# Transposing the input of a feed-forward stage on TensorE, or reading it turned from DRAM and sending the moments round through DRAM

## The reference

```python
def _layernorm(x, axis=-1, eps=1e-05):
    m = jnp.mean(x, axis=axis, keepdims=True)
    v = jnp.var(x, axis=axis, keepdims=True)
    return (x - m) / jnp.sqrt(v + eps)
...
    h = jnp.einsum('bsd,fd->bsf', x, w1q) + b1      # w1q, w2q: ternary weights
    h = jax.nn.gelu(h, approximate=False)
    return jnp.einsum('bsf,df->bsd', h, w2q) + b2
...
x = x + 0.5 * _L0_ffn_ref(_layernorm(x, axis=-1), w1, b1, w2, b2)
x = x + _L0_attn_ref(_layernorm(x, axis=-1), Wq, Wk, Wv, Wo)
x = x + 0.5 * _L0_ffn_ref(_layernorm(x, axis=-1), w1, b1, w2, b2)
```

## Time and profile before

| | us |
|---|---|
| median of 3 runs | 593.09 |
| lowest and highest | 592.05, 595.17 |
| the profiled execution | 596.39 |
| its span in the profile | 594.6 |
| first matmuls of chunks 1 to 7 start at | 37.45, 53.49, 69.53, 85.57, 101.59, 117.64, 133.67 |

### The profile page before, as it was taken

One profiled execution on the slowest core, in us unless ns is written; L12 is line 12 of the kernel. 1 busy time (PEld: TensorE's weight loads), 2 busy tenths in 40 slices (PEclk: granted clock), 3 DMA queues, 4 the chain that ended last, 5 costly groups with the idle time before them and its releaser, 6 DMA issues.

```text
span 594.6 us, 17184 instructions
## 1 busy us (share of the span) xinstructions
PE 557.4 (94%) x6404; PEld 486.8 (82%) x6404; DVE 453.0 (76%) x892; ACT 346.5 (58%) x614; POOL 240.3 (40%) x447
## 2 busy tenths in 40 slices
PE   1899999999789999999999999998889899999998
PEld 1789999999768888888888888886666888899997
DVE  4877777878787888889988898985654677777765
ACT  2754444556426767776766786776558265544443
POOL 5374333222745464554546465443321311333310
PEclk9999999999988999999999999998889799999999
DMA  7630000000776788877877877788412102111111
GB/s 211 213 112 7 0 0 0 0 0 1 212 214 191 241 245 247 244 231 222 249 255 242 263 240 226 236 251 260 129 67 73 39 6 102 36 35 35 35 36 37
DMA packets 88743, 80.97 MB, mean 136 GB/s; under 512 B 13522, under 2 KB 73714, under 8 KB 88690
## 3 DMA queue, kind: packets, MB, share of 16 engines
q1 hardware_dynamic: 82898, 71.73, 40.0%
q10 hardware_dynamic: 5792, 8.53, 3.9%
HBM read 41.68 MB, written 38.01 MB: 134 GB/s over the span
## 4 chain that ended last, share of the span: by engine, by line
PE 65%; DVE 9%; DMA 8%; POOL 5%; SPq 5%; ACT 4%; issue 3%; POOLq 0%; DVEq 0%; ACTq 0%
PE bank L569 19%; PE bank L180 18%; PE bank L1148 8%; PE bank L710 4%; PE bank L1143 4%; SPq L726 4%; PE bank L163 3%; PE bank L1208 3%; PE bank L800 3%; DMA qk_slots<-parts 2%; DMA den<-head_slots 2%; DVE mx L961 2%; POOL parts L908 2%; DMA q<-mt 1%; PE bank L1244 1%
## 5 line engine op out<-in xcount | busy, mean ns | idle before, releaser
L961 DVE TENSOR_REDUCE mx<-bank 128x2 f32<-128x512 f32 (+1 forms) x192 | 119.8, 683 | 19.0 <-PE bank L1148 18.5
L246 ACT ACTIVATE g<-bank,b1c 128x512 f32<-128x512 f32 x128 | 88.0, 690 | 71.8 <-PE bank L180 68.2
L569 PE MATMUL bank<-w2q,g_hi 128*128 128x256 f32 x512 | 125.7, 286 | 3.1 <-DVE g_lo L263 2.8
L569 PE MATMUL bank<-w2q,g_lo 128*128 128x256 f32 x512 | 123.8, 282 | 0.0
L1067 ACT ACTIVATE probs<-bank 128x512 f32<-128x512 f32 x192 | 110.8, 597 | 18.3 <-PE bank L1148 12.5
L569 PEld LDWEIGHTS bank<-w2q,g_hi 128*128 128x128 f32 x512 | 96.9, 189 | 5.1 <-DVE g_lo L263 2.5
L569 PEld LDWEIGHTS bank<-w2q,g_lo 128*128 128x128 f32 x512 | 96.9, 189 | 0.7
L325 POOL TENSOR_TENSOR res<-res,b2h 128x1024 f32 (+1 forms) x16 | 39.0, 2434 | 137.2 <-DVE xn L154 134.4
L263 DVE TENSOR_TENSOR g_lo<-g,g_hi 128x512 fp32r<-128x512 f32 x128 | 82.9, 686 | 3.8 <-ACT g_hi L250 0.5
L180 PE MATMUL bank<-xt_hi,w1q 128*128 128x512 f32 x240 | 77.7, 405 | 1.8 <-DVE xt_lo L174 1.8
L1148 PE MATMUL bank<-k,q 99*64 99x128 bf16 (+1 forms) x1024 | 77.2, 253 | 0.0
(11 more groups left out here) (125 smaller groups left out, 1075.3 us busy)
## 6 DMA issues: line engine op xcount, KB each, us to landing
qk_slots<-parts SPq DMA_DIRECT2D x32, 384.0 KB, 3.9
q<-qk_slots SPq DMA_DIRECT2D x32, 384.0 KB, 3.9
k<-qk_slots SPq DMA_DIRECT2D x32, 384.0 KB, 4.6
qk_slots<-parts SPq DMA_DIRECT2D x32, 256.0 KB, 3.5
head_slots<-o_sb ACTq DMA_DIRECT2D x32, 256.0 KB, 3.6
res<-x SPq DMA_DIRECT2D x8, 512.0 KB, 3.9
qk_slots<-parts SPq DMA_DIRECT2D x32, 128.0 KB, 4.6
att<-head_slots SPq DMA_DIRECT2D x16, 256.0 KB
```

Of the source, the lines that this page charges most:

```text
L246: nc.scalar.activation(g[:, f, :], of[:], ACT.Gelu, bias=b1c[:, f:f + 1]).then_inc(g_ready, 1)
L569: last = nc.tensor.matmul(to[:, 0:D], part[:, f, t * P:(t + 1) * P], w2q[:, f, :], start=f == 0 and part is g_hi, stop=f == FC - 1 and par ...
L961: nc.vector.tensor_reduce(o, i, AX.X, ALU.max).then_inc(s_done, 1)
```

## The change

Chunks 2 to 7 of the first feed-forward stage no longer get their turned input from TensorE. The host lays x out a second time by features (`xt_rows`, for each chunk 128 partitions of 2 x 512 numbers), and SP loads a chunk of it into `xn`. Statistics are still taken from `res`, where a row lies in one partition; in the turned layout each row is a column, so that its mean and rstd are needed in every partition. POOL's mean and rstd (128 partitions x 4 tiles) now lie in one tile `moment`; SP stores them in DRAM in the order of the rows, one element of 4 bytes at a time, and loads the 2 x 512 numbers back into all 128 partitions (`moments_b`). POOL subtracts and multiplies in place (`centre_rows`), ACT rounds from `xn` (`round_rows`), DVE subtracts (`split_rows`). For those chunks `ln_apply` on DVE and `transpose_x` on TensorE are gone. In POOL's loop the bias addition no longer waits for the normalised input. Chunks 0 and 1, the second feed-forward stage and the closing of chunk 7 stay as they were.

```diff
+TURNED = 2
+SKIPPED = CHUNKS - TURNED
...
+        moments_dram = nc.dram_tensor("moment_rows", (CHUNKS, 2, CN), F32, kind="Internal").ap()
...
-        mean = sb("mean", [P, CT])
+        moment = sb("moment", [P, 2, CT])
+        mean, rstd = moment[:, 0, :], moment[:, 1, :]
...
+        xn_rows = xn[:].rearrange("p t d -> p (t d)").rearrange("p (k s) -> p k s", k=KC)
+
+        def round_rows(act, n, hi=xt_hi):
+            act.wait_ge(xn_ready, CT * n + CT)
+            for k in range(KC):
+                nc.scalar.copy(hi[:, k, :], xn_rows[:, k, :]).then_inc(xt_hi_s, 1)
+
+        def split_rows(dve, n, hi=xt_hi, lo=xt_lo):
+            for k in range(KC):
+                dve.wait_ge(xt_hi_s, KC * n + k + 1)
+                nc.vector.tensor_tensor(lo[:, k, :], xn_rows[:, k, :], hi[:, k, :].bitcast(F32), ALU.subtract).then_inc(xt_lo_s, 1)
+
+        def centre_rows(pool, c, moments_b):
+            pool.wait_ge(xt_in, 16 * (c - TURNED + 1))
+            pool.wait_ge(moments_in, 16 * (c - TURNED + 1))
+            for i, op in enumerate((ALU.subtract, ALU.mult)):
+                if i:
+                    pool.wait_ge(centred, c - TURNED + 1)
+                pool.tensor_tensor(xn_rows, xn_rows, moments_b[:, i, :].unsqueeze(1).broadcast_to([P, KC, CN]), op)\
+                    .then_inc(xn_ready if i else centred, CT if i else 1)
...
                         sp.wait_ge(attw_in, 80)
+                        for c in range(TURNED, CHUNKS):
+                            sp.wait_ge(xt_lo_s, KC * c)
+                            sp.dma_start(xn_rows, xt_rows[c]).then_inc(xt_in, 16)
+                            sp.wait_ge(ln_rstd, 2 * c + 2)
+                            with nc.allow_non_contiguous_dma(reason="4 KiB in all"):
+                                for a in range(2):
+                                    sp.dma_start(moments_dram[c, a].rearrange("(t p) -> p t", p=P), moment[:, a, :])\
+                                      .then_inc(moments_out, 16)
+                            sp.wait_ge(moments_out, 32 * (c - TURNED + 1))
+                            sp.dma_start(moments_b[:], moments_dram[c].partition_broadcast(P)).then_inc(moments_in, 16)
+                        sp.wait_ge(xn_ready, CT * CHUNKS)
...
-                        pool.wait_ge(xn_ready, CT * (norm + c) + CT)
+                        if phase == 1 or isinstance(c, int):
+                            pool.wait_ge(xn_ready, CT * (norm + c) + CT)
...
                         moments(pool, c + norm)
                         residual(c)
+                        if phase == 0:
+                            centre_rows(pool, c, moments_b)
...
+                        by_rows = phase == 0 and not first and not closing
...
-                        elif following is not None:
+                        elif following is not None and not by_rows:
                             ln_apply(dve, following, n)
...
                                 if before:
-                                    split_xt(dve, n, last_hi, last_lo)
+                                    split_rows(dve, n, last_hi, last_lo)
+                                elif by_rows:
+                                    split_rows(dve, n)
...
-                            round_xt(act, c + norm + 1, to)
+                            if phase == 0 and not first:
+                                round_rows(act, c + norm + 1, to)
+                            else:
+                                round_xt(act, c + norm + 1, to)
...
-                        if more and not closing:
+                        if more and not closing and (phase == 1 or first):
                             transpose_x(pe, n + 1)
...
+        "xt_rows": inputs["L0_attn_x"].reshape(CHUNKS, CN, KC, P).transpose(0, 3, 2, 1),
```

More of the change, by code:

```diff
@@ L41, with macaron_kernel @@
 ROWS = SCORED + PARTS
-def macaron_kernel(nc, x, w1t, b1, w2t, b2, wqk, wv, wo, rope_cos, rope_sin, out):
+def macaron_kernel(nc, x, xt_rows, w1t, b1, w2t, b2, wqk, wv, wo, rope_cos, rope_sin, out):
     ctx = ExitStack()
@@ L85, in macaron_kernel @@
         variance = sb("variance", [P, CT])
-        mean = sb("mean", [P, CT])
+        moment = sb("moment", [P, 2, CT])
+        mean, rstd = moment[:, 0, :], moment[:, 1, :]
         minus_half = sb("minus_half", [P, CT])
-        rstd = sb("rstd", [P, CT])
         shift = sb("shift", [P, CT])
@@ L107, in macaron_kernel @@
         x0_shift = sem("x0_shift")
+        xt_in, moments_out, moments_in, centred = (sem(n) for n in ("xt_in", "moments_out", "moments_in", "xt_centred"))
         xt_ps, xt_hi_s, xt_lo_s = sem("xt_ps"), sem("xt_hi_s"), sem("xt_lo_s")
@@ L167, in round_xt @@
             for k in range(KC):
-                act.wait_ge(xt_ps, KC * n + k + 1)
+                act.wait_ge(xt_ps, KC * (n if isinstance(n, int) and n < TURNED else n - SKIPPED) + k + 1)
                 nc.scalar.copy(hi[:, k, :], banks[k][:]).then_inc(xt_hi_s, 1)
+        xn_rows = xn[:].rearrange("p t d -> p (t d)").rearrange("p (k s) -> p k s", k=KC)
[15 more added lines that the diff above has]
+                    .then_inc(xn_ready if i else centred, CT if i else 1)
         def split_xt(dve, n, hi=xt_hi, lo=xt_lo):
@@ L235, in feed_forward @@
                     b2f = sb("b2f", [P, D])
+                    moments_b = sb("moments_b", [P, 2, CN])
                     raw = [w1f[:].rearrange("p c f -> p (c f)"), w2f[:].rearrange("p c f -> p (c f)")]
```

## The result

| | before | changed |
|---|---|---|
| median of 4 runs each, same chip, us | 592.62 | 660.27 |
| lowest and highest | 592.05, 595.17 | 659.53, 662.77 |
| profiled execution and its span | 596.39, 594.6 | 659.53, 657.8 |

The changed kernel takes 1.112 times as long (95% interval 1.108 to 1.117): 67.7 us slower. The forecast was slower by 23, so its sign was right and its size was wrong; 660 lies outside its range of 602 to 636. In the job of the experiment with the centring on DVE, two of seven executions of the kernel before ran slow (600.06 and 772.79 us), and its median, 592.87, is that of the other five.

What follows compares the result with a forecast made beforehand. TensorE bounds the kernel before; a ring of waits through DRAM would bound the changed one. Chunk 2 late 6.2, five turns 13.2, closing 1.9 and clock 1.7 make +23 us: 616 us, range 602 to 636.

Steps and rivals of the forecast that it cites:

- the stores: Two stores of the moments to DRAM each turn: 2.8 us, with 2.3 for the second; ends 2.15 and 5.8.
- stores are dear: Rival: stores land as the slowest of the nearest row, 5.3 us, making the ring 21.7 and the kernel 634; 20%.
- The estimate of 2.5 us by that page's fit: Stores priced by the skill page's fit, 2.0 us plus bytes at 436 GB/s; with load 3.25, about 610 in all.
- The ring: From one chunk's split to the next, through statistics, moments, stores, load back, centring, cast: 18.7 us a turn against 16.04.
- centring: POOL's subtraction and multiplication of each chunk, 2.40 us each, with three hand-overs: 4.95 us in the ring.
- load back: Moments loaded from DRAM into all partitions, 512 KB: 3.95 us with the wake; ends 3.0 and 7.25.
- bias addition hidden: POOL's bias addition, 2.40 us, falls into the 6.75 us of DMA; uncovered, it would add 2.40 a chunk.
- The 0.8 for disturbed moments: In each turn, DVE's two-input subtractions beside the end of POOL's moments add 0.8 us; lower end 0.
- A lower end: All lower ends together: ring 16.13, chunk 2 at +4.5, five turns +0.5, closing 1.9, giving 600 us.
- TensorE's own period of 15.09: TensorE's work per chunk, 16.04 us, falls to 15.09 by removing 0.95 of transposes.
- the not-slower rival: Rival: the ring closes inside TensorE's 15.09; about 592, or 587 with chunk 2 in time too; 4%.
- Closing chunk and clock: In chunk 7, chunk 0's late normalising for attention adds 1.9 us and TensorE's lowered clock 1.7 (ends 0 and 3.4).

Runs made afterwards that it cites:

- the spread ones: Changed kernel with its 1024 stored 4-byte elements 512 or 64 bytes apart, rows of x loaded back in place of the moments: 623.36 and 617.02 us.
- the 64-byte run: Changed kernel with stored 4-byte elements 64 bytes apart, rows of x loaded back instead of moments: 617.02 us, +24.2 against the kernel before.
- the run with contiguous pieces: Changed kernel with moments stored in 16-byte pieces and x's columns reordered so POOL reads contiguously, ACT and DVE in strides: 631.63 us, +36.9 against before.

## Why the prediction was right and wrong

**The step that failed** is the stores: "Here the engines stand idle, so I take 2.3 for the second store, a little above the lowest because of the many pieces", with 5.3 (5.8 with the issue) as the upper end. From the second issue to the load back's issue it took 8.3 to 10.8 us, six times. The mean of the six, 9.5, in place of 2.3 adds 6 x 7.2 = 43 us, and 616 + 43 = 659, where 660.27 was measured. The row that I took as nearest has a quarter of the pieces at sixteen times the size, and I read its landing as a latency that hardly grows with the number of pieces. The doubled stores show a cost for each element, and the spread ones that it comes from adjacency, which no row of the trace before could show. The upper end should have allowed for a price that goes by the piece.

- **The rival "stores are dear"** named the right link; its price, 5.3, was still little more than half of what came.
- **The warning of the Trainium skill** that was weighed (DMA: Bandwidth & Descriptors, Rules for kernel authors, one descriptor for each element of a strided last dimension) was right. The estimate of 2.5 us by that page's fit, which the page gives for DMAs issued by GpSimd and not by SP, meets what the spread elements took (0.4 of issue and 2.0) and is a quarter of what the adjacent ones took.
- **The ring**, its order and all other terms held: statistics 1.32 (forecast 1.31), centring 4.8 (4.95), cast and split 2.0 (2.0), load back 4.2 in the median (3.95), bias addition hidden. With cheap stores the forecast's numbers came out: in the 64-byte run the split of chunk 2 ends at 59.71 (forecast 59.7), and the loss is 24.2 (23). That agreement is partly luck. Its period of 18.5 holds a centring of 5.85 us beside lows where the sum had 4.95 and 0.8 of disturbed moments.
- **The 0.8 for disturbed moments** did not come in the turns: they end at 72.47, and the first cast of DVE starts at 73.05.
- **A lower end** was mis-added: its ring of 16.13 takes 4.80 for the centring; with the sum's own 4.95 it is 16.28, and the end 601.
- **TensorE's own period of 15.09** was wrong: 15.72, since the residual additions show once the transposes are gone. I named no wait that would be late next there. In this result it costs nothing, but the not-slower rival's 587 was never to be had.
- **Closing chunk and clock**, 1.9 + 1.7, came to 2.4 together and are one term. The stretches of the changed kernel (busy us of PE, PEld, DVE, ACT, POOL; granted clock, DMA share, GB/s):

```profile
190.00:194.00 4.00, 0.00 (x0) 0.00 (x0) 1.03 (x2) 1.14 (x2) 2.28 (x1) 0.50 0.00 1
194.00:198.00 4.00, 3.64 (x9) 2.89 (x10) 2.23 (x7) 0.69 (x1) 2.02 (x7) 0.50 0.16 20
198.00:202.00 4.00, 4.00 (x20) 3.32 (x19) 3.40 (x9) 3.17 (x6) 0.37 (x2) 0.81 0.12 16
```

  TensorE had stood, then ran at 0.50 (1.2 of 2.4 GHz), and its first four groups took from 194.36 to 200.52, 6.16 us in place of 3.72. Chunk 0 was normalised at 199.86, ahead of that, so the two delays lie side by side.
- **POOL beside DVE** was weighed in one direction alone: DVE holding POOL's moments. That POOL, with two more whole-chunk instructions and a bias addition that no longer waited, would hold DVE's casts and lows was no rival. In the result it hides behind the stores: the centring runs after the lows of its chunk. It decides as soon as the stores are cheap.

**Still open**: the runs with pieces of 16 or 32 bytes lose 35 to 38 us, the two with spread elements 23 and 24, though the stores land as fast. In the former the centring meets the middle of the lows and TensorE is behind, in the latter it meets the last ones and TensorE waits for the split. The granted clock goes with that (0.82 to 0.91 from 60 to 160 us in the run with contiguous pieces, 1.00 from 80 in the 64-byte run). That the strided reading (1.1 us in place of 0.6 to 0.7 in cast and split, or 6.1 to 8.3 in place of 4.8 in the centring) tips it from the one into the other is only argued.

## What to carry to other kernels

Moments that must change from partitions to columns should go to DRAM in runs, or at least not as single elements side by side: price a store by its pieces and by where they land, not by its bytes. When work moves to GpSimd, list what VectorE runs at that time and where its inputs lie; a whole-tile instruction of GpSimd may cost VectorE its own length, unless VectorE reads one operand from PSUM. When it moves to VectorE instead, look at what then stands behind it and frees TensorE's banks. And when a piece goes from an engine's chain, look for the wait that it covered: of 0.95 us of transposes 0.3 was to be had.

## What the runs showed of the hardware, unexpected

- Stores of 4-byte elements to adjacent places took 8.2 to 10.8 us for 1024 and 15.9 to 18.3 for 2048; the same 1024 at 64 or 512 bytes from one another took 1.9 to 2.7.
- A subtraction of VectorE took up to 2.9 us in place of 0.68 beside one of GpSimd and ended 0.55 us behind GpSimd's. With one input in PSUM it took what it takes alone.
- Less DMA in the ring did not mean less time: with none of it the split of chunk 7 ended at 155.67 us, with 5.7 us of DMA a turn at 153.13.
